# A GRU-like recurrence on one core: TensorE's loop of four steps, x in column tiles, and the z gate of the second half in a group of its own

## The chip, the core and the metric

The program runs on one core of a Trainium2 chip. The metric is the device time of one execution in microseconds. Engines are named as in the profile: PE is TensorE (PEld its weight loads), DVE VectorE, ACT ScalarE, POOL GpSimd, SP the engine that issues the DMAs.

## What is computed

For a batch of 8 sequences of 512 steps with 512 features, all in float32:

```python
def step(h, x_t):
    fused = sigmoid(concatenate([x_t, h], -1) @ w_W + w_b)      # 1024 x 1024
    r, z = split(fused, 2, axis=-1)
    m = x_t @ wx_W + wx_b + r * (h @ wh_W + wh_b)               # 512 x 512 each
    h_new = z * h + (1.0 - z) * tanh(m)
    return (h_new, h_new)
out = x + scan(step, h0, x over time)
```

Each step needs the h of the step before it, so 512 steps follow one another. The products with x do not depend on h.

## The kernel before

The 512 features lie as 128 partitions x 4 chunks (`KC`); the four chunks are two halves (`HALVES`), 0 ("A") and 1 ("B"). A step's products with h are 3 gates (r, m, z) x 512 outputs. h is the stationary operand (128 rows x 8 columns, the batch), the weights `wh` move, and four column tiles of the array (`tile_position=(0, 32*j)`, `TILES` = 4) work at the same time, each on a quarter of the outputs. A matmul of the program on float32 is two matmuls and two weight loads in the trace.

The outputs are cut into groups, each in its own bank of `ps`, (first column, columns, bank): `RM_A` (r and m of half A, 128 columns), `RMZ_B` (r, m and z of half B, 192) and `Z_A` (z of half A, 64). A call `products(group, half, s)` adds the part of one half of h to a group; it is 8 matmuls of the program, 16 in the trace. PE's step is: wait for h of half A, RM_A and RMZ_B with half A of h; wait for half B of h, RM_A with half B (done: `rm_a_done`), Z_A with both halves (`z_a_done`), RMZ_B with half B (`rmz_b_done`). That is 96 matmuls in the trace, on line 192.

After it PE does some of the products with x, for the next block of 16 steps (`STEPS`). Here `wx` is stationary, 128 x 128 over the whole array, and x moves, 128 columns (16 steps x 8). `x_list` holds 48 of these per block, and `X_PLAN` gives 3 or 4 of them to each of the steps 0 to 14 and none to step 15; in the trace they are line 181, x6 or x8 a step. The address of x in `x_sb` depends on the loop's counter. ACT takes the finished units out of PSUM (line 228) and places a step's x part in `add` (line 233).

DVE's step, in order, with the trace's lines: turn (a 32x32 transpose out of PSUM) of r and m of A, line 284; `sum_r` (288); turn of z of A; `sum_z` (292); `mix_m` (298, a scan that gives r*(hW+b)+x); turn of r and m of B; `mix_h` of A (307, a scan that writes h and frees PE by `h_ready[0]`); `sum_r` of B; turn of z of B; `sum_z`, `mix_m`, `mix_h` of B (`h_ready[1]`). ACT answers with sigmoids (237, 241) and the tanh (246) that `mix_h` needs. POOL adds the bias to the m product (362) and makes y = x + h (375). Both `mix_m` wait for POOL and ACT, and both `mix_h` for ACT.

All engines run their own loop of 32 blocks of 16 steps written out. SP loads x for the block after the next and stores y once per block. Every engine executes its instructions in the order written; there is no scheduler.

Of the kernel before, what the change touches and what calls it, by code (L numbers as in the profile page):

```python
# [5 lines left out]
ALU = mybir.AluOpType  # L6
ACT = mybir.ActivationFunctionType

P = 128
# [3 lines left out]
def build(nc, x, h0, w_h, w_x, b_x, b_h, out):  # L13
# [6 lines left out]
    STEPS = 16  # L20
    BLOCKS = T // STEPS
    TOK = STEPS * B
    UNITS = HALVES * GATES * HC
    Y_HALF = STEPS // 2
# [7 lines left out]
    X_FROM = [-(-len(x_list) * s // (STEPS - 1)) for s in range(STEPS)] + [len(x_list)]  # L32
    X_PLAN = [x_list[X_FROM[s]:X_FROM[s + 1]] for s in range(STEPS)]
    X_ENDS = [[u for u, k in plan if k == KC - 1] for plan in X_PLAN]

# [3 lines left out]
    RMZ_B = (P, P + P // 2, 1)  # L39
    Z_A = (2 * P + P // 2, P // 2, 2)  # L40
    GROUP_BANKS = 3
# [12 lines left out]
    with ctx:  # L54
# [9 lines left out]
        x_sb = sb("x_sb", [P, KC, T * B])  # L64
        wx = sb("wx", [P, UNITS, KC, P])
# [5 lines left out]
        h = sb("h", [P, STEPS, HALVES, HALF])  # L71
        y = sb("y", [P, KC, STEPS, B])
# [13 lines left out]
        def h_of(s, k):  # L86
            o, ci = divmod(k, HC)
            at = 1 + TRI * B * ci + 1
            return h[:, s, o, at:at + TRI * (B - 1) + 1:TRI]
# [13 lines left out]
        x_loaded = sem("x_loaded")  # L103
        y_stored = sem("y_stored")
# [7 lines left out]
        rmz_b_done = sem("rmz_b_done")  # L112
# [4 lines left out]
        x_product = sem("x_product")  # L117
        r_summed = halves("r_summed")
# [20 lines left out]
        def _(sp):  # L139
            sp.sem_inc(y_stored, 16)  # L140
            x_flat = x.rearrange("p c t b -> p c (t b)")
            out_flat = out.rearrange("p c t b -> p c (t b)")
            sp.dma_start(x_sb[:, :, 0:TOK], x_flat[:, :, 0:TOK]).then_inc(x0_loaded, 16)  # L143
# [11 lines left out]
            def store(i):  # L155
                sp.wait_ge(y_added, sp.snap(i * STEPS + 2 * STEPS))
                sp.sem_inc(y_taken, 1)
                sp.dma_start(out_flat[:, :, bass.ds(sp.snap(i * TOK), TOK)],
                             y[:, :, :, :].rearrange("p c t b -> p c (t b)")).then_inc(y_stored, 16)

            with sp.Fori(0, BLOCKS - 2) as i:
                sp.wait_ge(x_loaded, sp.snap(i * 16 + 16))
                cols = bass.ds(sp.snap(i * TOK + 2 * TOK), TOK)
                sp.dma_start(x_sb[:, :, cols], x_flat[:, :, cols]).then_inc(x_loaded, 16)
                store(i)
            sp.wait_ge(x_loaded, (BLOCKS - 1) * 16)
            sp.sem_inc(x_loaded, 16)
            with sp.Fori(BLOCKS - 2, BLOCKS) as i:
                store(i)
            sp.wait_ge(y_stored, 16 * (BLOCKS + 1))  # L170

        @block.tensor
        def _(pe):
            def x_products(plan, i_next, unit0):
                for u, k in plan:
                    if k == 0 and not (isinstance(unit0, int) and unit0 + u < 2):
                        pe.wait_ge(xg_ready, unit0 + (u - 1))
                    cols = slice(0, TOK) if isinstance(i_next, int) else bass.ds(i_next * TOK, TOK)
                    if isinstance(i_next, int) and k == 0 and u * WX_PARTS % UNITS == 0:
                        pe.wait_ge(wx_loaded[u * WX_PARTS // UNITS], 16)  # L180
                    mm = pe.matmul(ps[:, X_BANK + u % 2, 0:TOK], wx[:, u, k, :], x_sb[:, k, cols],  # L181
                                   start=(k == 0), stop=(k == KC - 1))
                    if k == KC - 1:
                        mm.then_inc(x_product, 1)
# [256 lines left out]
```

## Time and profile before

| | us |
|---|---|
| median of 3 runs | 1894.34 (1892.4 to 1894.72) |
| the profiled execution, whole | 1895.98 |
| its span, first to last instruction | 1893.4 |
| PE busy (98% of the span) | 1859.9 |
| DVE busy (62%) | 1169.8 |
| ACT busy (43%) | 821.2 |
| POOL busy (20%) | 371.0 |

Of the profiled execution, 2.6 us lie outside the span. The granted TensorE clock has a mean of 0.998 over the span. A busy PE is a PE with a matmul in flight; several overlap, so that the share says little of how full the array is.

### The profile page before, as it was taken

Reading aid. Unit: us, or ns where it says so; the run is one execution under the profiler, and the core shown is the slowest. Engines: PE = TensorE matmul, PEld = TensorE weight load, DVE = VectorE, ACT = ScalarE, POOL = GpSimd, SP = SyncE. Lnnn points to the kernel's source line nnn. Section 1 sums busy time; section 2 is a strip of 40 time slices with the busy share of each in tenths; the row PEclk is TensorE's granted clock in tenths of the full one; section 3 lists DMA queues with packets and bytes.
Section 4 is the critical chain, followed back from the end, with each engine's and each line's share of the span. In section 5 each row is a group of like instructions: output and inputs, shape, how many; then the busy total and the mean of one; then the engine's idle time right before and its main releaser. Section 6 shows DMA issues by size and latency. Waiting matters only on the chain.

```text
span 1893.4 us, 124703 instructions
## 1 busy us (share of the span) xinstructions
PE 1859.9 (98%) x52320; PEld 1465.7 (77%) x52320; DVE 1169.8 (62%) x6153; ACT 821.2 (43%) x3983; POOL 371.0 (20%) x1540
## 2 busy tenths in 40 slices
PE   8999999999999999999999999999999999999998
PEld 6777777777777777777777777777777777777776
DVE  3666666666666666666666666666666666666665
ACT  3444444444444444444444444444444444444444
POOL 0111111111111111111111111111111111111111
PEclk9999999999999999999999999999999999999999
DMA  4000000000000000000000000000000000000000
GB/s 152 15 4 15 15 15 15 9 9 15 15 15 15 4 15 15 15 15 4 15 15 15 15 9 9 15 15 15 15 4 15 15 15 15 4 15 15 9 9 9
DMA packets 36083, 29.94 MB, mean 16 GB/s; under 512 B 1616, under 2 KB 34384, under 8 KB 35664
## 3 DMA queue, kind: packets, MB, share of 16 engines
q1 hardware_dynamic: 35664, 23.10, 3.9%
q8 instruction: 416, 6.82, 1.5%
q14 instruction: 3, 0.02, 0.0%
HBM read 14.70 MB, written 8.39 MB: 12 GB/s over the span
## 4 chain that ended last, share of the span: by engine, by line
PE 96%; DVE 2%; DMA 1%; ACT 1%; SPq 0%; issue 0%; POOL 0%; POOLq 0%
PE ps L192 73%; PE ps L181 23%; DVE turned L284 1%; DMA x_sb<-in_x 1%; DVE h L307 0%; ACT h_by L241 0%; DVE pre_z L292 0%; DVE pre_r L288 0%; ACT h L246 0%; SPq L146 0%; SPq L152 0%; SPq L143 0%; SPq L150 0%; SPq L148 0%; SPq L149 0%
## 5 line engine op out<-in xcount | busy, mean ns | idle before, releaser
L192 PE MATMUL ps<-wh,h 128*8 128x128 f32 (+2 forms) x49152 | 1443.2, 273 | 22.5 <-DVE h L307 19.2
L192 PEld LDWEIGHTS ps<-wh,h 128*8 128x8 f32 x49152 | 1073.4, 90 | 260.1 <-DVE h L307 44.0
L284 DVE STREAM_TRANSPOSE turned<-ps 128x128 f32<-128x128 f32 (+1 forms) x2048 | 575.1, 281 | 510.6 <-PE ps L192 483.6
L237 ACT ACTIVATE m_by<-pre_r 128x16 f32<-128x16 f32 x1024 | 223.4, 218 | 894.5 <-DVE pre_r L288 894.5
L181 PEld LDWEIGHTS ps<-x_sb,wx 128*128 128x128 f32 x3168 | 392.3, 192 | 161.8 <-issue 161.8
L181 PE MATMUL ps<-x_sb,wx 128*128 (+1 forms) x3168 | 483.9, 292 | 5.6 <-DMA wx<-in_w_x 5.6
L362 POOL TENSOR_TENSOR add<-turned,bias_h 128x16 f32<-128x16 f32 x1024 | 237.4, 232 | 881.4 <-DVE turned L284 881.4
L307 DVE TENSOR_TENSOR_SCAN h<-h_by,h 128x48 f32<-128x48 f32 x1024 | 263.5, 257 | 152.9 <-ACT h L246 152.6
L241 ACT ACTIVATE h_by<-pre_z 128x16 f32<-128x16 f32 x1024 | 230.2, 225 | 160.0 <-DVE pre_z L292 131.2
L375 POOL TENSOR_TENSOR y<-x_sb,h 128x32 f32<-128x32 f32 x512 | 133.4, 261 | 637.5 <-DVE h L307 637.5
L246 ACT ACTIVATE h<-m_pre 128x32 f32<-128x32 f32 x1024 | 237.6, 232 | 0.0
L298 DVE TENSOR_TENSOR_SCAN m_pre<-m_by,add 128x32 f32<-128x32 f32 x1024 | 224.7, 219 | 0.0
L292 DVE TENSOR_TENSOR pre_z<-turned,add 128x16 f32<-128x16 f32 x1024 | 179.6, 175 | 35.0
L288 DVE TENSOR_TENSOR pre_r<-turned,add 128x16 f32<-128x16 f32 x1024 | 167.1, 163 | 17.4
L228 ACT ACTIVATE xg<-ps,bias_x 128x128 f32 (+1 forms) x396 | 145.5, 367 | 9.3 <-PE ps L181 9.1
L233 ACT ACTIVATE add<-xg 128x96 f32 (+1 forms) x513 | 145.5, 284 | 0.1
L338 DVE MEMSET ps<- 128x1536 f32 x1 | 1.3, 1338 | 1.2 <-PEq L433 1.2
L350 DVE COPY h<-h 128x8 f32<-128x8 f32 x4 | 0.4, 168 | 2.5 <-DMA h<-in_h 2.5
L267 ACT ACTIVATE warm<-bias_h 128x4 f32<-128x4 f32 x1 | 0.2, 205 | 3.8 <-DMA bias_h<-in_b_h 3.8
L267 ACT ACT_TABLE_LOAD x1 | 1.3, 1283 | 0.7 <-PEq L433 0.7
L341 DVE MEMSET h<- 128x1600 f32 x1 | 1.4, 1392 | 0.3 <-issue 0.3
L433 POOL MEMSET const-float32-0.0<- 128x1 f32 x1 | 0.1, 99 | 0.2 <-issue 0.2
(6 smaller groups left out, 0.6 us busy)
## 6 DMA issues: line engine op xcount, KB each, us to landing
x_sb<-in_x SPq DMA_DIRECT2D x32, 256.0 KB, 4.6
out_h<-y SPq DMA_DIRECT2D x32, 256.0 KB, 2.7
wx<-in_w_x SPq DMA_DIRECT2D x6, 512.0 KB, 5.8
wh<-in_w_h SPq DMA_DIRECT2D x4, 768.0 KB, 11.3
bias_x<-in_b_x SPq DMA_DIRECT2D x1, 6.0 KB, 3.2
bias_h<-in_b_h SPq DMA_DIRECT2D x1, 2.0 KB, 3.1
h<-in_h SPq DMA_DIRECT2D x1, 16.0 KB, 3.6
```

The costliest lines, as they stand in the source:

```text
L181: mm = pe.matmul(ps[:, X_BANK + u % 2, 0:TOK], wx[:, u, k, :], x_sb[:, k, cols], start=(k == 0), stop=(k == KC - 1))
L192: mm = pe.matmul(ps[Q * j:Q * j + B, bank, 0:cols], h_of(s - 1 if s else S, k), wh[:, k, j, at:at + cols], start=(k == 0), stop=(k == KC - 1),
L228: act.activation(dst, ps[:, X_BANK + u % 2, 0:TOK].rearrange("p (t b) -> p t b", b=B), ACT.Identity, bias=bias_x[:, u:u + 1]).then_inc(xg_ ...
L237: act.activation(m_by[:, o, :, 1], pre_r[:, o, :], ACT.Sigmoid).then_inc(r_ready[o], 1)
L241: act.activation(h_by[:, o, :, 2], pre_z[:, o, :], ACT.Sigmoid).then_inc(z_ready[o], 1)
L246: act.activation(n_twice, m_pre[:, o, :, 1].unsqueeze(2).to_broadcast([P, HB, 2]), ACT.Tanh)\
L284: return dve.transpose(turned[:, o, g0:g1].rearrange("p g c q -> p (g c) q"), ps[:, bank, at:at + cols].rearrange("p (c q) -> p c q", q=Q))
L288: dve.tensor_tensor(pre_r[:, o].rearrange("p (c b) -> p c b", b=B), product_of(o, R), x_of(par, o, R), ALU.add).then_inc(r_summed[o], 1)
L292: dve.tensor_tensor(pre_z[:, o].rearrange("p (c b) -> p c b", b=B), product_of(o, Z), x_of(par, o, Z), ALU.add).then_inc(z_summed[o], 1)
L298: dve.tensor_tensor_scan(m_pre[:, o].rearrange("p i w -> p (i w)"), m_by[:, o].rearrange("p i w -> p (i w)"), add[:, par, o, M].rearrange( ...
L307: dve.tensor_tensor_scan(h[:, s, o, 0:REGION], h_by[:, o].rearrange("p i w -> p (i w)"), h[:, s - 1 if s else S, o, 1:1 + REGION], 0.0, AL ...
L362: pool.tensor_tensor(add[:, par, o, M, :, 0].rearrange("p (c b) -> p c b", b=B), product_of(o, M), bias_h[:, HC * o:HC * (o + 1)].unsqueez ...
```

## The change

PE's loop is four steps (`RING` = 4) and runs 128 times, where it was sixteen steps and ran 32 times. All addresses in it are fixed: the x weights of each step come by DMA into one of four places `wx_step` (three 128 x 128 blocks a step, 192 KB), the x of the next block lies four times in `x_next`, and h is a ring of four. SP issues these loads: one `wx_step` each step, and one `x_next` in each of the last four steps of a block. y gets two buffers. Each step has exactly three x products, step 15 too, and each is four matmuls in column tiles of 32 stationary columns, the cut that the products with h have. The x units go round three PSUM banks instead of two.

`RMZ_B` is split into `RM_B` (128 columns) and `Z_B` (64 columns, bank 3). PE computes Z_B last, both halves after RM_B is done. DVE does `sum_r` of B ahead of `mix_h` of A, and turns z of B after it. DVE waits for POOL's y additions every four steps, and for all of them up to the step before; it was every eight, with eight steps of lag. POOL waits for the load of `x_sb` at each block's start, where PE did.

The diff, cut to its core:

```diff
-    X_FROM = [-(-len(x_list) * s // (STEPS - 1)) for s in range(STEPS)] + [len(x_list)]
-    X_PLAN = [x_list[X_FROM[s]:X_FROM[s + 1]] for s in range(STEPS)]
+    X_EACH = len(x_list) // STEPS
+    X_UNITS = RING * X_EACH // KC
...
-    RMZ_B = (P, P + P // 2, 1)
-    Z_A = (2 * P + P // 2, P // 2, 2)
+    RM_B = (P, P, 1)
+    Z_A = (2 * P, P // 2, 2)
+    Z_B = (2 * P + P // 2, P // 2, 3)
...
+            for r in range(RING):
+                load_wx(r)
+                sp.dma_start(x_next[:, r], x_flat[:, :, TOK:2 * TOK]).then_inc(x_next_loaded[r], 16)
             sp.dma_start(x_sb[:, :, TOK:2 * TOK], x_flat[:, :, TOK:2 * TOK]).then_inc(x_loaded, 16)
...
+            def x_product_of(u, k, w, moving):
+                for j in range(TILES):
+                    at = slice(Q * j, Q * (j + 1))
+                    mm = pe.matmul(ps[at, X_BANK + u % X_UNITS, 0:TOK], w[:, at], moving,
+                                   start=(k == 0), stop=(k == KC - 1), tile_position=(0, Q * j))
...
+            def x_products(i, s):
+                pe.wait_ge(wx_step_loaded[s], held(pe, i * 16 + 16))
+                pe.wait_ge(x_next_loaded[s], held(pe, (i // (STEPS // RING)) * 16 + 16))
+                for n in range(X_EACH):
+                    u, k = divmod(s * X_EACH + n, KC)
+                    if k == 0:
+                        pe.wait_ge(xg_ready, held(pe, i * X_UNITS + (UNITS - X_UNITS + u + 1)))
+                    last = x_product_of(u, k, wx_step[:, s, n, :], x_next[:, s, k, :])
...
                 pe.wait_ge(h_ready[0], nxt)
                 products(RM_A, 0, s)
-                pe.wait_ge(z_b_turned, nxt)
-                products(RMZ_B, 0, s)
+                products(RM_B, 0, s)
                 pe.wait_ge(h_ready[1], nxt)
                 products(RM_A, 1, s).then_inc(rm_a_done, 1)
                 products(Z_A, 0, s)
                 products(Z_A, 1, s).then_inc(z_a_done, 1)
-                products(RMZ_B, 1, s).then_inc(rmz_b_done, 1)
+                products(RM_B, 1, s).then_inc(rm_b_done, 1)
+                pe.wait_ge(z_b_turned, nxt)
+                products(Z_B, 0, s)
+                products(Z_B, 1, s).then_inc(z_b_done, 1)
...
-            with nc.Fori(0, BLOCKS, engines=(mybir.EngineType.PE,), hint_back_edge=True) as i:
+            with nc.Fori(0, T // RING, engines=(mybir.EngineType.PE,), hint_back_edge=True) as i:
...
-                if s % Y_HALF == 0:
-                    dve.wait_ge(y_added, held(dve, t0 + (s + Y_HALF)))
+                if s % RING == 0:
+                    dve.wait_ge(y_added, held(dve, t0 + (s + STEPS)))
...
+                pool.wait_ge(x_loaded, pool.snap(i * 16 + 16))
```

PE, one step inside the loop. Before (step 1 of the block; `8x192` is a matmul with 8 stationary and 192 moving columns, in the program's own count, half of the trace's):

```order
L192 MATMUL ps<-wh,h 8x128 [waits h_ready0]
L192 MATMUL ps<-wh,h 8x128 x7
L192 MATMUL ps<-wh,h 8x192 [waits z_b_turned]
L192 MATMUL ps<-wh,h 8x192 x7
L192 MATMUL ps<-wh,h 8x128 [waits h_ready1]
L192 MATMUL ps<-wh,h 8x128 x7
L192 MATMUL ps<-wh,h 8x64 x16
L192 MATMUL ps<-wh,h 8x192 x8
```

After, the last step of the loop's body with the loop's end:

```order
L232 MATMUL ps<-wh,h 8x128 [waits h_ready0]
L232 MATMUL ps<-wh,h 8x128 x15
L232 MATMUL ps<-wh,h 8x128 [waits h_ready1]
L232 MATMUL ps<-wh,h 8x128 x7
L232 MATMUL ps<-wh,h 8x64 x16
L232 MATMUL ps<-wh,h 8x128 x8
L232 MATMUL ps<-wh,h 8x64 [waits z_b_turned]
L232 MATMUL ps<-wh,h 8x64 x15
L200 MATMUL ps<-x_next,wx_step 32x128 [waits x_next_loaded3,wx_step_loaded3]
L200 MATMUL ps<-x_next,wx_step 32x128 x11
L256 REGISTER_ALU
L256 COMPARE_AND_BRANCH
```

The 64 columns of z of B moved from the 192-column matmuls to the end, and the branch now stands behind x products. Before, the branch stood right behind step 15's products with h, and step 0 began with a wait for h:

```order
L192 MATMUL ps<-wh,h 8x64 x16
L192 MATMUL ps<-wh,h 8x192 x8
L213 REGISTER_ALU
L213 COMPARE_AND_BRANCH
L54 UNCONDITIONAL_BRANCH
```

DVE, middle of a step, before:

```order
L298 SCALAR_TENSOR_TENSOR m_pre<-m_by,add 128x32 [waits hm_ready0,r_ready0]
L284 STREAM_TRANSPOSE turned<-ps 128x128 [waits rmz_b_done]
L307 SCALAR_TENSOR_TENSOR h<-h_by,h 128x48 [waits z_ready0,tanh_ready0]
L288 TENSOR_TENSOR pre_r<-turned,add 128x16 [waits rm_b_turned]
L284 STREAM_TRANSPOSE turned<-ps 128x64
```

and after:

```order
L338 SCALAR_TENSOR_TENSOR m_pre<-m_by,add 128x32 [waits hm_ready0,r_ready0]
L324 STREAM_TRANSPOSE turned<-ps 128x128 [waits rm_b_done]
L328 TENSOR_TENSOR pre_r<-turned,add 128x16 [waits rm_b_turned]
L347 SCALAR_TENSOR_TENSOR h<-h_by,h 128x48 [waits z_ready0,tanh_ready0]
L324 STREAM_TRANSPOSE turned<-ps 128x64 [waits z_b_done]
```

`pre_r` of B moved ahead of the h of A, and the last turn waits for a group of its own.

## Rows read from the trace of the kernel before

**Rows 1.** the page: span, first part, and the instruction queue of part 3
```profile
span 1893.4 us, 124703 instructions
...
PE 1859.9 (98%) x52320; PEld 1465.7 (77%) x52320; DVE 1169.8 (62%) x6153; ACT 821.2 (43%) x3983; POOL 371.0 (20%) x1540
...
q8 instruction: 416, 6.82, 1.5%
```

**Rows 2.** the chain of work in time, 901.4 to 920: start us, us, what
```profile
901.51 1.09 PE ps L181 x8
902.60 2.74 PE ps L192 x96
905.34 0.86 PE ps L181 x6
```

**Rows 3.** waits, whole run: engine line, waited for, us in total, times, longest us
```profile
PEld ps L181 <- issue: 161.8, 481, 5.6
```

**Rows 4.** timeline of a covered step: start us, us, what [idle before]
```profile
905.27 0.74 PEld L181 LDWEIGHTS ps<-x_sb,wx 128*128 128x128 f32 x6 [0.33 <-issue]
...
906.13 2.81 PE L192 MATMUL ps<-wh,h 128*8 128x128 f32 x96
...
907.91 0.32 DVE L284 STREAM_TRANSPOSE turned<-ps 128x128 f32<-128x128 f32 x1 [0.88 <-PE ps L192]
...
908.88 0.94 PE L181 MATMUL ps<-x_sb,wx 128*128 x6
```

**Rows 5.** timeline of the uncovered step, 897 to 900.5, same columns
```profile
897.01 0.32 DVE L284 STREAM_TRANSPOSE turned<-ps 128x128 f32<-128x128 f32 x1 [0.88 <-PE ps L192]
897.36 0.18 DVE L288 TENSOR_TENSOR pre_r<-turned,add 128x16 f32<-128x16 f32 x1
...
897.46 0.25 DVE L284 STREAM_TRANSPOSE turned<-ps 128x64 f32<-128x64 f32 x1
...
897.83 0.22 DVE L298 TENSOR_TENSOR_SCAN m_pre<-m_by,add 128x32 f32<-128x32 f32 x1
...
898.08 0.23 ACT L246 ACTIVATE h<-m_pre 128x32 f32<-128x32 f32 x1
898.11 0.32 DVE L284 STREAM_TRANSPOSE turned<-ps 128x128 f32<-128x128 f32 x1
898.35 0.26 DVE L307 TENSOR_TENSOR_SCAN h<-h_by,h 128x48 f32<-128x48 f32 x1
...
898.52 0.15 DVE L288 TENSOR_TENSOR pre_r<-turned,add 128x16 f32<-128x16 f32 x1
898.59 0.24 DVE L284 STREAM_TRANSPOSE turned<-ps 128x64 f32<-128x64 f32 x1
...
898.66 2.85 PE L192 MATMUL ps<-wh,h 128*8 128x128 f32 x96 [0.62 <-DVE h L307]
...
899.47 0.26 DVE L307 TENSOR_TENSOR_SCAN h<-h_by,h 128x48 f32<-128x48 f32 x1 [0.30 <-ACT h L246]
899.78 1.33 PEld L192 LDWEIGHTS ps<-wh,h 128*8 128x8 f32 x64 [0.24 <-DVE h L307]
899.97 0.27 POOL L375 TENSOR_TENSOR y<-x_sb,h 128x32 f32<-128x32 f32 x1 [1.22 <-DVE h L307]
...
900.48 0.32 DVE L284 STREAM_TRANSPOSE turned<-ps 128x128 f32<-128x128 f32 x1 [0.75 <-PE ps L192]
```

**Rows 6.** back edge, by line: durations min/median/max ns, first and last start
```profile
L213 PEldq ALU_OP  x1: 32/32/32, 897.2 to 897.2; - x1
L213 PEldq COMPARE_BRANCH  x1: 375/375/375, 897.3 to 897.3; - x1
...
L199 PEldq ALU_OP  x1: 36/36/36, 897.9 to 897.9; - x1
...
L353 DVEq COMPARE_BRANCH  x1: 61/61/61, 899.6 to 899.6; - x1
```

**Rows 7.** timeline: the second half's h of the first and the last step
```profile
28.92 0.26 DVE L307 TENSOR_TENSOR_SCAN h<-h_by,h 128x48 f32<-128x48 f32 x1 [0.30 <-ACT h L246]
...
1889.44 0.26 DVE L307 TENSOR_TENSOR_SCAN h<-h_by,h 128x48 f32<-128x48 f32 x1 [0.30 <-ACT h L246]
```

**Rows 8.** the page, part 6: KB each, median us from issue to landing
```profile
wx<-in_w_x SPq DMA_DIRECT2D x6, 512.0 KB, 5.8
```

More of the change, by code:

```diff
@@ L20, in build @@
     STEPS = 16
+    RING = 4
     BLOCKS = T // STEPS
@@ L103, in build @@
         x_loaded = sem("x_loaded")
+        x_next_loaded = [sem(f"x_next_loaded{r}") for r in range(RING)]
+        wx_step_loaded = [sem(f"wx_step_loaded{r}") for r in range(RING)]
         y_stored = sem("y_stored")
@@ L117, in build @@
         x_product = sem("x_product")
+        x_used = [sem(f"x_used{r}") for r in range(RING - 1)]
         r_summed = halves("r_summed")
@@ L167, in _ @@
[L167 to L170, printed above, removed]
+                             y[:, bass.ds(sp.snap(i % 2), 1)].rearrange("p a c t b -> p (a c) (t b)"))\
+                    .then_inc(y_stored, 16)
+            sp.wait_ge(x_loaded, (BLOCKS + 1) * 16)
+            for r in range(RING):
+                sp.wait_ge(wx_step_loaded[r], (T // RING + 1) * 16)
+                sp.wait_ge(x_next_loaded[r], (BLOCKS + 1) * 16)
@@ L172, in _ @@
+            sp.wait_ge(y_stored, 16 * (BLOCKS + 2))
         @block.tensor
         def _(pe):
[L174 to L179, printed above, removed]
-                        pe.wait_ge(wx_loaded[u * WX_PARTS // UNITS], 16)
[L181 to L184, printed above, removed]
+            def x_product_of(u, k, w, moving):
[3 more added lines that the diff above has]
+                                   start=(k == 0), stop=(k == KC - 1), tile_position=(0, Q * j))
+                if k == KC - 1:
+                    mm.then_inc(x_product, 1)
+                return mm
@@ new lines, in first_x_products @@
+            def first_x_products():
+                for u, k in x_list:
+                    if k == 0 and u >= X_UNITS:
+                        pe.wait_ge(xg_ready, u - X_UNITS + 1)
+                    if k == 0 and u * WX_PARTS % UNITS == 0:
+                        pe.wait_ge(wx_loaded[u * WX_PARTS // UNITS], 16)
+                    x_product_of(u, k, wx[:, u, k, :], x_sb[:, k, 0:TOK])
+            def x_products(i, s):
[6 more added lines that the diff above has]
+                    last = x_product_of(u, k, wx_step[:, s, n, :], x_next[:, s, k, :])
+                if s < RING - 1:
+                    last.then_inc(x_used[s], 1)
@@ L364, in hidden, with add_x @@
                     .then_inc(hm_ready[o], 1)
-            def add_x(s, t0, nxt, after):
+            def add_x(s, t0, which, after):
                 if s == 0:
@@ L382, in step @@
                     hidden(o, s % 2, nxt)
-                add_x(s, t0, nxt, held(pool, t0 + (s + 2)))
+                add_x(s, t0, which, held(pool, t0 + (s + 2)))
             pool.sem_inc(y_added, STEPS)
```

97 lines of the change are left out of this document (54 added, 43 removed).

## The prediction, made before the changed kernel ran

> **What bounds the kernel now.** I read the page first: PE has a matmul in flight for 98% of the span, the other engines are far below [rows 1]. Then the chain of waits in order of time: it runs through PE for step after step, 2.74 us of products with h and 0.86 us of products with x, 3.60 us a step, or 0.86 + 0.23 where eight x matmuls stand instead of six [rows 2]. So PE sets the pace of 15 of 16 steps. The span holds 511 steps between the end of the first h of half B (28.92 + 0.26 = 29.18) and of the last (1889.70) [rows 7]: 1860.5 / 511 = 3.641 us a step. Around them lie 29.2 us at the start, 1893.4 - 1889.7 = 3.7 at the end and 1895.98 - 1893.4 = 2.6 outside the span.
>
> The row that matters most is the one step that PE does not bound. Step 15 has no x products, so PE stands idle 0.62 us for the h of half A [rows 5]. From one turn of r and m of A to the next it takes 900.48 - 897.01 = 3.47 us. That is the length of the recurrence itself: turn, sum, sigmoid, scan, tanh, scan, for A and then B, and PE's products back to the turn. Whatever PE gains, the step does not get under this loop unless the loop changes too. The slack is 3.641 - 3.47 = 0.17 us a step, 87 us in all.
>
> **PE's own time.** x in column tiles. Before each x phase the weight loader stands idle 0.33 us [rows 4], 481 times and 161.8 us in total [rows 3], for no semaphore: with the array full of column tiles the first full-width load waits. In the chain [rows 2], eight x matmuls take 1.09 us and six 0.86, so one costs (1.09 - 0.86) / 2 = 0.115 us, six cost 0.69, and 0.17 of the 0.86 is the switch; some 0.12 more hides in the end of the 2.74, as drain. With x in the cut of the h products both go. The six become 24 of 32 columns, in sets of four that stream the same 128 columns: 0.69 us, if four loads of 32 columns cost together what one of 128 does. The h products keep their 384 columns per part of h; 32 more matmuls in the trace cost a few ns each. PE alone: 2.74 + 0.69 = 3.43 at most, 3.31 if the drain of 0.12 is gone. I take 3.31. Step 15 now has its x products too, and the eights become sixes. So PE falls below the recurrence of 3.47, and the recurrence becomes the bound.
>
> The Trainium skill has a sentence on this, in "TensorEngine Tiling (Array Packing)", section "Key Properties": changing the tiling mode, not only the tile, drains the engine. The trace has the 0.33 us in front of every change to full width, and nothing of the kind between h groups.
>
> **The recurrence after the change.** I write T for the start of the turn of r and m of A and walk along DVE's order with the intervals of [rows 5]. Before: `sum_r` at 0.35, turn of z at 0.45, `mix_m` at 0.82, turn of B at 1.10, h of A at 1.34 (the tanh ends at 1.30), `sum_r` of B 1.51, turn of z of B 1.58, h of B 2.46, its end 2.72, next turn 3.47, which is 0.75 us after the end of h.
> After, up to `mix_m` nothing changes: RM_A and Z_A are done at the same distance. The turn of B comes earlier. It stood at 1.10 since the 192-column products of `RMZ_B` ended then; with 128 columns they end 0.2 us earlier (a third of 16 matmuls at 2.74 / 12288 us per column: 1024 columns, 0.23). Then the scan `mix_m` is the bound: DVE starts an instruction about 0.08 before the end of the one ahead if it waits for nothing (898.59 against 898.52 + 0.15), so 0.82 + 0.22 - 0.08 = 0.96. `sum_r` of B waits for all of that turn: 0.96 + 0.35 = 1.31. Now h of A stands behind it: 1.31 + 0.10 = 1.41, not 1.34, a loss of 0.07. The turn of z of B follows 0.17 behind h of A (898.52 - 898.35), at 1.58; before, `sum_r` stood between and it was 1.58 too. Gain and loss cancel, and from there nothing changes: h of B ends at 2.72, the next turn is at 3.47. If the turn of B stays at 1.10, as an upper bound, everything after it shifts by 0.14 and the step is 3.61, a gain of almost nothing.
>
> Z_B stands last on PE and is no wait: before, 5120 columns stood behind RM_A and x began 908.88 - 907.91 = 0.97 after T, the drain in it [rows 4]. Now it is 6144 columns: 1024 more are 0.22, and the drain of 0.12 goes or stays, so x begins at T + 1.07 to 1.19, and z of B is turned at 1.58. x ends at 1.76 to 1.88. RM_A and RM_B with half A of h are a third of the h products, 0.87 to 0.91, and end at 2.63 to 2.79; h of B is there at 2.72 and its first load starts 0.05 later (899.78). The two meet almost at one time. PE then waits 0 to 0.14 us a step, and the steps have little cover left for anything late on PE.
>
> **The back edge.** The loop turns 128 times instead of 32. PE's sequencer takes from 897.2 to 897.9 + 0.04 for it, 375 ns of that in the branch, where DVE's takes 61 [rows 6]. Before, this lay under the wait for h. It was begun when the matmuls of the last group, 16, were still ahead of the array. With the same lead, it begins now 16 matmuls of x (0.44 to 0.46 us) before the end of x, at about T + 1.31; 0.77 us later PE can take the first matmul, at 2.1 to 2.15 with its start, and with 0.88 for RM_A and RM_B it is ready for h of B at 3.02 instead of 2.79: 0.23 us an edge, 127 edges, 29 us. The lower bound: the instruction queue moved 6.82 MB, which is 65 bytes for each of the 104,640 matmuls and loads that PE executed and only 55 for each of all 124,703 instructions [rows 1]. I read that as PE's loop fetched anew each time round, and the other engines' smaller loops kept. If PE's short loop is kept too and the branch costs what DVE's does, the edge takes 0.3 less and costs 0 to 0.05 us: 0 to 6 us. Nothing in the trace shows which, so I take the middle, 0.14 us, 18 us in all. The Trainium skill ("Runtime: NRT & Kernel Launch", section "Instruction fetch mechanics") gives PE room for 2048 instructions; by that the new loop of some 1,250 would fit and the old one of some 3,300 would not, if what was fetched is kept at all, and the sum would be 1809 to 1815. The same section calls that memory a FIFO without a cache's reuse, by which the edge would cost as before or more.
>
> **The rest.** DVE waits every four steps for the y addition of the step before. POOL starts it 899.97 - (899.47 + 0.26) = 0.24 after h of B and takes 0.27; it is done 0.51 after h, the turn is at 0.75. Cover 0.24, cost 0; it would take a POOL half as slow again to show. SP issues one load a step more, three of them ahead, so that each has some 10 us, where 512 KB land in 5.8 [rows 8]: 0. At the start `x_sb` of block 1 is queued behind 1.8 MB more and POOL waits for it, but PE no longer does; I set 0, with 0 to 5 us for the range. At the end, the last loads stand before the store: 0 to 1 us.
>
> **Sum.** 29.2 + 511 x 3.47 + 18 + 3.7 + 2.6 = 29.2 + 1773.2 + 24.3 = 1826.7 us, against 1895.98 of the profiled execution, which lies 1.6 above the median. Rounded with that: 1826.
>
> **Rivals.**
> *The turn of B doesn't come early enough*: it stays between 0.96 and 1.10, since the order on DVE or the end of RM_B holds it. The steps take 3.54 to 3.61 and PE has slack that hides the back edge: 29.2 + 511 x 3.61 + 6.3 = 1880, or 1850 in the middle. For it: DVE now stands idle nowhere between `mix_m` and h of A. Against: RM_B's end is reckoned at 0.9. Chance 0.18.
> *PE still bounds and the recurrence gets shorter*, by something that I put down as fixed: 29.2 + 511 x 3.31 + 6.3 = 1727, plus edges. Against it speaks that every interval in the loop was seen at 3.47 with no PE in the way. 0.05.
> *Slower by the loads of column tiles.* If a load of 32 columns isn't hidden behind its own tile's matmuls, a set of four takes 0.11 + 0.11 us, the x phase 1.3 instead of 0.69 and PE 3.93: 29.2 + 511 x 3.93 + 6.3 = 2044. It decides from 0.17 us a set on, where PE reaches 3.64. Against: the narrow loads of 8 columns are hidden even behind 64-column matmuls. 0.08.
> *Slower by the fetch at the back edge.* The instruction queue was busy 1.5% of 16 engines' span for 416 packets, 1.1 us each [rows 1]. If every edge stalls for one such packet beyond the 0.77 us seen, it costs 0.23 + 1.1 = 1.33 us, 169 in all: 1809 + 169 = 1978. It decides from 0.68 us an edge on, where 127 edges eat the 87 us. Against: the branch of before went as far back and took 375 ns. 0.06. The same section of the Trainium skill has the rule: a taken branch to a place outside the window that is held forces a fetch before the engine goes on.
> That the change doesn't do what it says (the loads of `wx_step` late, PE waiting for them) I give 0.01; it would be seen as waits for DMA.
>
> **How the numbers follow.** The forecast (recurrence 3.47, edge 0 to 0.23, some us at the start) holds 0.62 and gives 1808 to 1845. The first rival takes it on to 1880. Together 0.80, so the range is 1806 to 1882. What it leaves out is 0.15 above and 0.05 below. A measurement can tell about 0.2% from no change, 3.8 us. Faster: 0.62 + 0.18 + 0.05, less 0.01 for a first rival that eats the whole gain: 0.84. Slower: 0.08 + 0.06 + 0.01 = 0.15. Same: 0.01; I give it 0.02 and faster 0.83.
>
> **What the new profile would show.** The 0.33 us of idle weight loader before x gone, and no idle time above 0.1 there. PE's waits for the h of half B in nearly each step, up to 0.14 us, and DVE and ACT in the chain of every step. Turn to turn 3.47 in three steps of four and 3.5 to 3.7 in the one with the branch. The turn of B 0.96 after the turn of A, h of A at 1.41. The instruction queue tells which edge it is: some tens of packets (kept) or some 600. Wrong would be: PE with no waits (a set of four above 0.15 us, or something on PE that I don't see), turn B at 1.1, or DVE waiting for POOL's y.

## The result, and the profile after

| | before | after |
|---|---|---|
| median | 1893.87 us (4 runs) | 1808.78 us (4 runs, 1807.97 to 1809.14) |
| ratio | | 0.9551 (0.9534 to 0.9567) |
| span of the profiled run | 1893.4 | 1806.1 |
| matmuls in the trace | 52,320 | 78,208 |
| mean step, from the end of the first h of B to the end of the last | 3.641 | 3.464 |

The kernel is 4.5% faster, 85 us. The prediction was 1826 with a range of 1806 to 1882, and its sum without the price for the back edge was 1809; 1808.78 lies 3 us inside the lower end of that range. The page, for [rows 1]:

```profile
span 1806.1 us, 178513 instructions
...
PE 1787.5 (99%) x78208; PEld 1629.9 (90%) x78208; DVE 1160.5 (64%) x6153; ACT 824.9 (46%) x3983; POOL 357.1 (20%) x1540
...
q8 instruction: 7, 0.11, 0.0%
...
PE 98%; SPq 1%; DMA 0%; issue 0%; DVE 0%; ACT 0%; POOL 0%; POOLq 0%; DVEq 0%
```

PE has half as many matmuls again and is as busy by this count as before. The instruction queue moved 7 packets where it had moved 416. The chain is PE's at 98%, and that is misleading: it follows PE back at nearly every joint, since PE and the h of B arrive nearly together there. The prediction had expected DVE and ACT in the chain of every step, and that sign did not come. What sets the pace is seen in the timeline of one step, DVE and PE (start us, us, what [idle before]), the counterpart of [rows 5]:

```profile
902.87 0.32 DVE L324 STREAM_TRANSPOSE turned<-ps 128x128 f32<-128x128 f32 x1 [0.82 <-PE ps L232]
903.22 0.17 DVE L328 TENSOR_TENSOR pre_r<-turned,add 128x16 f32<-128x16 f32 x1
...
903.31 0.24 DVE L324 STREAM_TRANSPOSE turned<-ps 128x64 f32<-128x64 f32 x1
...
903.68 0.22 DVE L338 TENSOR_TENSOR_SCAN m_pre<-m_by,add 128x32 f32<-128x32 f32 x1
...
903.82 0.29 DVE L324 STREAM_TRANSPOSE turned<-ps 128x128 f32<-128x128 f32 x1
...
903.99 0.60 PEld L200 LDWEIGHTS ps<-x_next,wx_step 128*32 128x32 f32 x24
...
904.15 0.18 DVE L328 TENSOR_TENSOR pre_r<-turned,add 128x16 f32<-128x16 f32 x1
...
904.24 0.28 DVE L347 TENSOR_TENSOR_SCAN h<-h_by,h 128x48 f32<-128x48 f32 x1
...
904.44 0.22 DVE L324 STREAM_TRANSPOSE turned<-ps 128x64 f32<-128x64 f32 x1
...
904.67 2.90 PE L232 MATMUL ps<-wh,h 128*8 128x128 f32 x128
...
905.30 0.26 DVE L347 TENSOR_TENSOR_SCAN h<-h_by,h 128x48 f32<-128x48 f32 x1 [0.29 <-ACT h L286]
...
905.61 1.78 PEld L232 LDWEIGHTS ps<-wh,h 128*8 128x8 f32 x96 [0.17 <-DVE h L347]
...
906.31 0.32 DVE L324 STREAM_TRANSPOSE turned<-ps 128x128 f32<-128x128 f32 x1 [0.75 <-PE ps L232]
```

From T = 902.87: turn of B at 0.95, `sum_r` of B at 1.28, h of A at 1.37, turn of z of B at 1.57, h of B at 2.43, the next turn at 3.44. The weight loader waits 0.17 us for the h of B (905.61) after RM_A and RM_B with half A; there is no idle time in front of the x products any more, where it was 0.33 [rows 4]. Between 100 and 1700 us, some 460 steps, the waits are (engine, for whom, us in total, times, longest):

```profile
PEld ps L232 <- DVE h L347: 102.2, 492, 0.3
PEld ps L200 <- issue: 3.3, 22, 0.2
```

The first row is the new wait, 492 waits of 0.21 us, 0.22 us a step, where the prediction had at most 0.14. The second stands for the 161.8 us of [rows 3], and is down to 3.3.

The back edge, for [rows 6] (duration in ns min/median/max, first and last start):

```profile
L256 PEldq COMPARE_BRANCH  x115: 216/216/216, 112.1 to 1689.2; - x115
```

The branch takes 216 ns where it took 375.

### The profile page after: what moved, and what is told of

Read it like the earlier page. It is cut to its first block, busy times and chain, and to the rows that moved or that the text cites. A ratio compares the mean times of both kernels' runs of the same rounds, so it can differ in the third digit from the quotient of the medians.

```text
span 1806.1 us, 178513 instructions
## 1 busy us (share of the span) xinstructions
PE 1787.5 (99%) x78208; PEld 1629.9 (90%) x78208; DVE 1160.5 (64%) x6153; ACT 824.9 (46%) x3983; POOL 357.1 (20%) x1540
## 4 chain that ended last, share of the span: by engine, by line
PE 98%; SPq 1%; DMA 0%; issue 0%; DVE 0%; ACT 0%; POOL 0%; POOLq 0%; DVEq 0%
PE ps L232 78%; PE ps L200 20%; SPq L167 0%; SPq L162 0%; DMA x_sb<-in_x 0%; SPq L153 0%; SPq L159 0%; DVE turned L324 0%; SPq L150 0%; DVE h L347 0%; DVE m_pre L338 0%; SPq L157 0%; SPq L156 0%; SPq L155 0%; DVE pre_r L328 0%
## 5 line engine op out<-in xcount | busy, mean ns | idle before, releaser
L232 PE MATMUL ps<-wh,h 128*8 128x128 f32 (+1 forms) x65536 | 1504.7, 246 | 2.6 <-issue 2.2
L232 PEld LDWEIGHTS ps<-wh,h 128*8 128x8 f32 x65536 | 1324.7, 90 | 143.1 <-DVE h L347 113.5
L324 DVE STREAM_TRANSPOSE turned<-ps 128x128 f32<-128x128 f32 (+1 forms) x2048 | 550.4, 269 | 412.4 <-PE ps L232 412.4
L200 PE MATMUL ps<-x_next,wx_step 128*32 128x128 f32 x12288 | 433.0, 274 | 0.6 <-issue 0.6
L403 POOL TENSOR_TENSOR add<-turned,bias_h 128x16 f32<-128x16 f32 x1024 | 222.8, 218 | 709.9 <-DVE turned L324 681.5
L200 PEld LDWEIGHTS ps<-x_next,wx_step 128*32 128x32 f32 x12288 | 316.1, 110 | 16.2 <-issue 4.3
L416 POOL TENSOR_TENSOR y<-x_sb,h 128x32 f32 x512 | 134.0, 262 | 734.5 <-DVE h L347 734.5
L328 DVE TENSOR_TENSOR pre_r<-turned,add 128x16 f32<-128x16 f32 x1024 | 179.8, 176 | 34.9
L200 PE MATMUL ps<-x_sb,wx 128*32 128x128 f32 x384 | 15.1, 323 | 9.8 <-DMA wx<-in_w_x 6.1
L200 PEld LDWEIGHTS ps<-x_sb,wx 128*32 128x32 f32 x384 | 13.3, 131 | 11.0 <-issue 10.3
```

What stands on the lines that cost most here:

```text
L200: mm = pe.matmul(ps[at, X_BANK + u % X_UNITS, 0:TOK], w[:, at], moving, start=(k == 0), stop=(k == KC - 1), tile_position=(0, Q * j))
L232: mm = pe.matmul(ps[Q * j:Q * j + B, bank, 0:cols], h_of(s - 1, k), wh[:, k, j, at:at + cols], start=(k == 0), stop=(k == KC - 1), tile_po ...
L324: return dve.transpose(turned[:, o, g0:g1].rearrange("p g c q -> p (g c) q"), ps[:, bank, 0:cols].rearrange("p (c q) -> p c q", q=Q))
L328: dve.tensor_tensor(pre_r[:, o].rearrange("p (c b) -> p c b", b=B), product_of(o, R), x_of(par, o, R), ALU.add).then_inc(r_summed[o], 1)
L403: pool.tensor_tensor(add[:, par, o, M, :, 0].rearrange("p (c b) -> p c b", b=B), product_of(o, M), bias_h[:, HC * o:HC * (o + 1)].unsqueez ...
```

## The experiments

All times stand against the kernel before, which ran beside each of them: 1893 to 1895 us. The first variant reads the x of block 0 in every block, so that the x part of its result is that of block 0 from the second block on; PE's number of products is the same. All others compute the whole result.

### The parts one at a time

**Column tiles alone**, on the kernel before:

```diff
-                    mm = pe.matmul(ps[:, X_BANK + u % 2, 0:TOK], wx[:, u, k, :], x_sb[:, k, cols],
-                                   start=(k == 0), stop=(k == KC - 1))
+                    for j in range(TILES):
+                        at = slice(Q * j, Q * (j + 1))
+                        mm = pe.matmul(ps[at, X_BANK + u % 2, 0:TOK], wx[:, u, k, at], x_sb[:, k, 0:TOK],
+                                       start=(k == 0), stop=(k == KC - 1), tile_position=(0, Q * j))
```

> The kernel before, with one edit: the x products go in four column tiles of 32. [...] No split of z of B, no short loop, no new loads. Theory (the full-width x cost PE the switch, and with it gone the recurrence bounds): steps with three x products 3.47 us, the three of 16 with four 3.54, mean 3.49, so 29.2 + 511 x 3.49 + 6.3 = 1819 us (1810 to 1828), the 0.33 us of idle weight loader before x gone. Rival (the gain of the change comes from the split of z and DVE's order, or from the short loop): 1880 to 1894. Rival (narrow loads aren't hidden): over 1900.

Measured: 1953.06 us, ratio 1.0285 (1.025 to 1.0319). Slower. A rival had "over 1900", but for loads that aren't hidden; the trace shows another reason. The page (span, instruction queue), PE's timeline where its loop turns, and the branch (ns):

```profile
span 1953.4 us, 143583 instructions
...
q8 instruction: 514, 8.42, 1.7%
```

```profile
928.80 3.05 PE L194 MATMUL ps<-wh,h 128*8 128x128 f32 x93 [2.40 <-issue]
```

```profile
L215 PEldq COMPARE_BRANCH  x2: 2392/2584/2777, 925.7 to 984.2; - x2
```

PE stands 2.4 us with no semaphore to wait for, and its branch takes 2.6 us instead of 0.375. From one end of h of B to the next, most steps of a block took 3.48 to 3.65 us, as the theory wanted, so the loads of the column tiles are hidden. But the first step of a block, behind the branch, took 5.2 to 7.3 (median 6.35), and some others up to 4.2: mean 3.755. The queue moved 514 packets in 1953.4 us, one in 3.80. My reading was that PE waits for its own instructions. The next run changes nothing but the length of the loop's body.

**The changed kernel with PE's body written out for 16 steps:**

```diff
-            with nc.Fori(0, T // RING, engines=(mybir.EngineType.PE,), hint_back_edge=True) as i:
-                t0 = pe.snap(i * RING)
-                for s in range(RING):
-                    step(t0, s)
-                    x_products(i, s)
+            with nc.Fori(0, BLOCKS, engines=(mybir.EngineType.PE,), hint_back_edge=True) as b:
+                for turn in range(STEPS // RING):
+                    t0 = pe.snap(b * STEPS + turn * RING)
+                    for s in range(RING):
+                        step(t0, s)
+                        x_products(b, turn, s)
```

> The changed kernel with PE's loop body written out for 16 steps instead of four, 32 turns instead of 128; every matmul, wait and place is the same. The instruction queue should go from 7 packets to about 610 (10 MB). Theory (the fetch and the edge lie under other work): 1803 to 1813 us, no change. Rival (the short loop is part of the gain: PE waits for its instructions, or an edge that has to be fetched again costs the 0.23 us that I feared): 1815 us for 31 edges of 0.23 us, more if the fetch between them stalls, since 304 instructions a step are half as many again as before.

Measured: 2506.95 us (2478.94 to 2521.22 in four runs), ratio 1.3254 (1.3192 to 1.3315). The same matmuls, waits and loads cost 700 us more. The page, and PE's waits between 100 and 1700 us:

```profile
span 2477.1 us, 178193 instructions
...
q8 instruction: 642, 10.52, 1.7%
```

```profile
PEld ps L232 <- issue: 367.2, 347, 3.5
```

The loop turns only 21 times in that window, so nearly all of the 347 waits lie inside the body and not at the branch: it is the stream of instructions that is late. 642 packets in 2477.1 us are one in 3.86, with the other loads beside them nearly the same as without (3.80 in the run before). PE executes 156,416 matmuls and loads from 642 packets, 244 from each. At the 3.80 us of the run before, a step of 304 needs 304 / 244 x 3.80 = 4.73 us, and the mean step was 4.78. The kernel before needed a packet in 1893.4 / 416 = 4.55 us and lived 16% under that limit. Column tiles for x alone need 514 packets for 512 steps; at 3.6 us a step that would be one in 3.6, and they are over it.

**The short loop alone**: four steps in PE's body with fixed places and the loads, x in full width, z of B not split and DVE in its old order. Against the changed kernel, cut:

```diff
-                for j in range(TILES):
-                    at = slice(Q * j, Q * (j + 1))
-                    mm = pe.matmul(ps[at, X_BANK + u % X_UNITS, 0:TOK], w[:, at], moving,
-                                   start=(k == 0), stop=(k == KC - 1), tile_position=(0, Q * j))
+                mm = pe.matmul(ps[:, X_BANK + u % X_UNITS, 0:TOK], w, moving,
+                               start=(k == 0), stop=(k == KC - 1))
...
-    RM_B = (P, P, 1)
-    Z_A = (2 * P, P // 2, 2)
-    Z_B = (2 * P + P // 2, P // 2, 3)
+    RMZ_B = (P, P + P // 2, 1)
+    Z_A = (2 * P + P // 2, P // 2, 2)
```

> The kernel before with only the short loop: PE's body has four steps with fixed places and the loads that this needs, x in full width, no split of z of B, DVE's old order. Theory (the short loop gives no time itself, it only makes room for more instructions): PE bounds at 2.74 + 0.86 = 3.60 us or a little more, 1878 to 1892 us, as the kernel with the split but full-width x. Rival (the fetch cost the kernel before something too): below 1870.

Measured: 1881.89 us, ratio 0.994 (0.9925 to 0.9955). A small gain, but its interval leaves out 1. The chain of waits in time shows the pair of before [rows 2], unchanged:

```profile
903.22 0.86 PE ps L196 x6
904.09 2.74 PE ps L228 x96
```

So the short loop itself gives 12 us. The steps say from what: before, three of 16 took 3.83 us (four x products) and one 3.47 (none), and the mean was 3.64; now every step has three, and the mean is 3.61. Above all it is what lets PE have more instructions. With the split but x still in full width (the first piece of that diff alone):

> The changed kernel with x in full width again, 128 stationary columns at a time from the same fixed places; the rest (short loop, ring, split of z of B, loads) stays. Theory: PE needs 2.74 + 0.86 = 3.60 us a step and bounds again, PE idle before x 0.33 us, time 31 + 511 x 3.60 + 7.5 = 1878 us (1865 to 1890). Rival (the split or the short loop made the gain): 1809 to 1830.

Measured: 1892.41 us, ratio 0.9989 (0.9979 to 0.9999); the steps took 3.63 us. PE bounds, as expected, but the time lies outside the expected 1865 to 1890: where PE bounds, the split costs 0.02 us a step, 10.5 us in all against the run above. Without the column tiles the short loop's 12 us and this loss leave almost nothing. Then without the split, with column tiles, the short loop and DVE's old order (cut):

```diff
-                products(RM_B, 1, s).then_inc(rm_b_done, 1)
-                pe.wait_ge(z_b_turned, nxt)
-                products(Z_B, 0, s)
-                products(Z_B, 1, s).then_inc(z_b_done, 1)
+                products(RMZ_B, 1, s).then_inc(rm_b_done, 1)
```

> The changed kernel without the split: r, m and z of B in one group of 192 columns, DVE with h of A ahead of sum_r of B, as before; x in column tiles and the short loop stay. Theory: the recurrence has its old length of 3.475 us where the changed kernel's has 3.444, turn of B at 1.10 instead of 0.96 after the turn of A: 1809 + 511 x 0.03 = 1824 us (1818 to 1832). Rival (the split is worth nothing, PE or another bound holds the 3.44): 1809. Rival (the split is worth much, since PE without it is late for h of B): over 1840.

Measured: 1823.76 us, ratio 0.9622 (0.9606 to 0.9638). 3.475 us in most steps, the length of the uncovered step of before. The parts, added in this order, make up the 85 us: the short loop 12 (1893.87 to 1881.89), the column tiles on it 58 (to 1823.76), the split with its order on DVE 15 (to 1808.78). The column tiles are most of the gain, and without the short loop they are a loss of 58.

And the split with DVE's old order, h of A ahead of `sum_r` of B:

```diff
+                mix_h(0, s, nxt)
                 dve.wait_ge(rm_b_turned, nxt)
                 sum_r(1, par, nxt)
-                mix_h(0, s, nxt)
```

> The changed kernel with h of A ahead of sum_r of B on DVE, as before; the groups of 128 and 64 columns stay. Theory (what the split gives is the earlier turn of B, and the new order of the two is worth nothing): turn of B at 0.96, h of A at 1.34, sum_r of B at 1.51, turn of z of B at 1.58 after the turn of A, as in the changed kernel: 1809 us within 4. Rival (the order is what counts): 1815 to 1825, as without the split.

Measured: 1853.29 us, ratio 0.9785 (0.977 to 0.98). My theory fell, and so did the rival's number: it is 44 us worse than the changed kernel and 30 worse than no split. The timeline:

```profile
901.27 0.32 DVE L324 STREAM_TRANSPOSE turned<-ps 128x128 f32<-128x128 f32 x1 [0.75 <-PE ps L232]
...
902.23 0.29 DVE L324 STREAM_TRANSPOSE turned<-ps 128x128 f32<-128x128 f32 x1
...
902.60 0.22 POOL L403 TENSOR_TENSOR add<-turned,bias_h 128x16 f32<-128x16 f32 x1 [0.71 <-DVE turned L324]
902.62 0.32 DVE L347 TENSOR_TENSOR_SCAN h<-h_by,h 128x48 f32<-128x48 f32 x1
902.85 0.14 DVE L328 TENSOR_TENSOR pre_r<-turned,add 128x16 f32<-128x16 f32 x1
902.92 0.24 DVE L324 STREAM_TRANSPOSE turned<-ps 128x64 f32<-128x64 f32 x1
...
904.81 0.32 DVE L324 STREAM_TRANSPOSE turned<-ps 128x128 f32<-128x128 f32 x1 [0.75 <-PE ps L232]
```

The turn of B is early, at 0.96, and h of A starts at 1.35, but that scan takes 0.32 us where it took 0.26 in [rows 5], and `sum_r` starts 0.23 behind it instead of 0.17. The turn of z of B comes at 1.65, and the step is 3.54.

What makes the scan longer stands on POOL. Since the turn of B is earlier now, POOL's bias addition for B falls on h of A: it starts 0.02 us ahead of the scan. In step 9 of each block the two start almost together, the scan first:

```profile
916.84 0.26 DVE L347 TENSOR_TENSOR_SCAN h<-h_by,h 128x48 f32<-128x48 f32 x1
916.84 0.28 POOL L403 TENSOR_TENSOR add<-turned,bias_h 128x16 f32<-128x16 f32 x1 [0.73 <-DVE turned L324]
917.02 0.15 DVE L328 TENSOR_TENSOR pre_r<-turned,add 128x16 f32<-128x16 f32 x1
```

There the scan takes 0.26 us and the addition 0.28 instead of 0.22, `sum_r` follows in 0.18, and the step is 3.483 instead of 3.54. It is so in 31 steps. In 448 the addition starts just ahead and the scan takes 0.31; in 31 more it starts earlier, and the scan begins 0.05 later and takes 0.26. Whichever of the two comes second ends about 0.06 late. In the changed kernel the addition starts about 0.05 ahead of the scan, which then takes 0.28. So 0.06 of the 0.10 that a step loses is this meeting of two engines. No run moved POOL's addition alone, and what the two share inside the chip is not shown.

### How large a loop may be

Two bodies written out for eight steps: that of the short loop alone (204 matmuls and loads a step), and that of the changed kernel (304). Both have this edit:

```diff
-            with nc.Fori(0, T // RING, engines=(mybir.EngineType.PE,), hint_back_edge=True) as i:
+            with nc.Fori(0, T // RING // 2, engines=(mybir.EngineType.PE,), hint_back_edge=True) as b:
+                for turn in range(2):
```

> The kernel with the short loop alone (x in full width, no split), with PE's body written out for eight steps: about 204 matmuls and loads a step, some 1,650 instructions in the body. It asks how large a body is kept. Theory (a room of 2048 instructions, as the Trainium skill has it for PE, is a cache here): the instruction queue moves 3 to 10 packets and the time stays at 1882 us. Rival (what is kept is less, somewhere above the 1,250 of the changed kernel): over 400 packets, and 1882 to 1900 us, since the kernel before lived with that rate.

Measured: 1883.44 us (one run), with 6 packets:

```profile
q8 instruction: 6, 0.10, 0.0%
```

> The changed kernel with PE's body written out for eight steps: 304 matmuls and loads a step, some 2,450 instructions. Theory (the body is over 2048 and the fetch rate of one packet of 256 instructions in 3.7 to 3.8 us bounds): about 610 packets, 304 / 67 = 4.5 us a step at least, 2300 to 2520 us like the body of 16. Rival (bodies of this size are still kept): under 10 packets and 1809 us.

Measured: 2526.16 us (one run, span 2523.7), with 642:

```profile
q8 instruction: 642, 10.52, 1.9%
```

A body of 204 x 8 = 1,632 matmuls and loads stays, one of 304 x 8 = 2,432 is fetched each time round. The 2048 instructions that the Trainium skill gives for PE ("Runtime: NRT & Kernel Launch", section "Instruction fetch mechanics") lie between the two. The same section calls that memory a FIFO, without a cache's gain from code that lies close together, and says that the pace at which the engine's instructions are issued hides the fetch. Here a body of 1,632 was not fetched again (6 packets in the whole run), and with one of 2,432 PE stood waiting for its instructions.

### How much room PE has

More x products in each step, into a bank that nothing reads, ahead of the second x product of each step (EXTRA is 2):

```diff
+                    for j in range(EXTRA * TILES if n == 1 else 0):
+                        at = slice(Q * (j % TILES), Q * (j % TILES + 1))
+                        pe.matmul(ps[at, 7, 0:TOK], wx_step[:, s, n, at], x_next[:, s, k, :],
+                                  start=True, stop=True, tile_position=(0, Q * (j % TILES)))
```

> The changed kernel with eight more column-tiled matmuls (two sets of four, 0.11 us each) in every x phase, into a bank that nobody reads; it measures how much PE has left under the recurrence. Theory (PE alone takes 3.31 us, the recurrence 3.444): the step becomes 3.31 + 0.22 = 3.53, 1809 + 511 x 0.07 = 1845 us. Rival (PE and the recurrence are in series, no slack): 1809 + 511 x 0.22 = 1921. Rival (PE has more slack than I think): 1809 to 1820.

Measured: 1964.61 us (one run). The edit put in twice what the expectation counted: eight float32 matmuls of the program are sixteen in the trace, four sets of 0.109 us. PE's timeline, with its products with h (L237) and the first of those with x (L201):

```profile
902.77 2.83 PE L237 MATMUL ps<-wh,h 128*8 128x128 f32 x128
905.53 0.43 PE L201 MATMUL ps<-x_next,wx_step 128*32 128x128 f32 x8
...
906.64 2.83 PE L237 MATMUL ps<-wh,h 128*8 128x128 f32 x128
909.28 0.41 PE L201 MATMUL ps<-x_next,wx_step 128*32 128x128 f32 x8
...
910.37 2.83 PE L237 MATMUL ps<-wh,h 128*8 128x128 f32 x128
...
914.10 2.83 PE L237 MATMUL ps<-wh,h 128*8 128x128 f32 x128
...
917.83 2.83 PE L237 MATMUL ps<-wh,h 128*8 128x128 f32 x128
```

The profile lists no wait of PE or its loader between 100 and 1700 us here, so PE alone sets the step. It is 3.73 us in three steps of four (910.37 - 906.64). 3.73 - 4 x 0.109 = 3.29: that is PE alone, where the prediction had 3.31. The changed kernel's step of 3.444 leaves it 0.15. The last step of the loop's body holds the branch, and it too takes 3.73 (917.83 - 914.10): the back edge costs nothing even where PE bounds. The long step is the first of the body, 3.87 (906.64 - 902.77): its x products begin 2.76 us after the products with h, in the others 2.64. In the changed kernel it is the same, 1.20 after the turn of A against 1.08. There PE's sequencer has register instructions for the values of three waits (lines 215, 216 and 220) ahead of the x products, in the other steps a single wait. That these cause the delay was not tried alone.

### The waits for y

Three steps of each block (4, 8 and 12) take 3.508 us where the others take 3.444. End of h of B to the next turn, first such a step, then the first step of a block:

```profile
929.41 0.26 DVE L347 TENSOR_TENSOR_SCAN h<-h_by,h 128x48 f32<-128x48 f32 x1 [0.30 <-ACT h L286]
930.49 0.32 DVE L324 STREAM_TRANSPOSE turned<-ps 128x128 f32<-128x128 f32 x1 [0.82 <-PE ps L232]
```

```profile
915.63 0.26 DVE L347 TENSOR_TENSOR_SCAN h<-h_by,h 128x48 f32<-128x48 f32 x1 [0.30 <-ACT h L286]
916.64 0.32 DVE L324 STREAM_TRANSPOSE turned<-ps 128x128 f32<-128x128 f32 x1 [0.75 <-PE ps L232]
```

929.67 to 930.49 is 0.82 us, 915.89 to 916.64 is 0.75. The second has the back edge of PE and the wait for y as well, so neither explains the difference. In the trace DVE's sequencer first passes the wait for `rm_a_done` as an instruction of its own and the turn carries the wait for y; in the first step of a block it is the other way round, since there the y wait rides on a register instruction. The semaphore that comes last costs 0.07 us more if it stands ahead of the turn and not on it.

```diff
-                if s % RING == 0:
-                    dve.wait_ge(y_added, held(dve, t0 + (s + STEPS)))
                 dve.wait_ge(rm_a_done, nxt)
...
+                if s % RING == 0:
+                    dve.wait_ge(y_added, held(dve, t0 + (s + STEPS)))
                 dve.wait_ge(rm_b_done, nxt)
```

> The changed kernel with DVE's wait for POOL's y additions moved from the start of every fourth step to the turn of r and m of B in the same step, where the ring place it guards is still untouched. In the changed kernel the steps 4, 8 and 12 of a block are 0.065 us longer than their neighbours (3.508 against 3.444), since the turn starts 0.82 us after h of B and not 0.75; in steps 0 it is 0.75. Theory (two waits on one instruction, the later one in front of it): the 96 long steps go to 3.444, 96 x 0.065 = 6 us, 1802.5 us. Rival (POOL's addition itself, or PE's back edge, makes these steps long): no change, 1809, or the delay shows at the turn of B.

Measured: 1812.85 us, ratio 0.957 (0.9557 to 0.9583). The expected 6 us did not come; it is 4 us worse than the changed kernel. The turn of A came 0.75 behind h in all steps, as the theory has it. But in four steps of each block the turn of B now started 0.03 late and took 0.02 more, though both its semaphores had long been set, so that `sum_r` of B was 0.05 late. The second wait costs DVE 0.05 us even where nothing is waited for, if DVE has no gap there. Four steps of 0.05 cancel three of 0.065. The other loss is in step 9 of each block: it takes 3.54 us instead of 3.46, with `mix_m` of A 0.09 late, 32 x 0.08 = 2.6 us. Why is open.

### A kernel that beats both

On DVE, the turn of z of B ahead of h of A:

```diff
-                mix_h(0, s, nxt)
                 dve.wait_ge(z_b_done, nxt)
                 turn(3, 1, Z, GATES).then_inc(z_b_turned, 1)
+                mix_h(0, s, nxt)
```

> The kernel with the y wait moved, and DVE's turn of z of B ahead of h of A: turn of B, sum_r of B, turn of z of B, h of A. Theory (DVE's order sets the recurrence): turn of z of B at 1.38 after the turn of A instead of 1.58, h of A at 1.51 instead of 1.38, sum_z of B at 1.68 instead of 1.83, m of B at 1.77 (its sigmoid is ready at 1.75), h of B ends at 2.55 instead of 2.69. Then h of A, ending at 1.79, and PE bound: 1.84 + 1.56 = 3.40 us a step, 1802.5 - 511 x 0.045 = 1780 us (1765 to 1795). Rival (h of A later makes PE later by as much as B gains): 1800 or above.

Measured: 1780.31 us, ratio 0.9401 (0.9389 to 0.9414), expected 1780. That the number fits so well is luck in part: the expectation started from 1802.5, but the kernel that it builds on took 1812.85, so the gain is 32.5 us where 22.5 was expected. Most steps take 3.38 us, not 3.40; the four with the y wait take 3.44.

```profile
899.88 0.32 DVE L324 STREAM_TRANSPOSE turned<-ps 128x128 f32<-128x128 f32 x1 [0.86 <-PE ps L232]
...
900.84 0.29 DVE L324 STREAM_TRANSPOSE turned<-ps 128x128 f32<-128x128 f32 x1
...
901.26 0.24 DVE L324 STREAM_TRANSPOSE turned<-ps 128x64 f32<-128x64 f32 x1
901.43 0.22 DVE L347 TENSOR_TENSOR_SCAN h<-h_by,h 128x48 f32<-128x48 f32 x1
...
902.15 0.26 DVE L347 TENSOR_TENSOR_SCAN h<-h_by,h 128x48 f32<-128x48 f32 x1 [0.30 <-ACT h L286]
903.27 0.32 DVE L324 STREAM_TRANSPOSE turned<-ps 128x128 f32<-128x128 f32 x1 [0.86 <-PE ps L232]
```

Turn of B at 0.96, turn of z 1.38, h of A 1.55, end of h of B 2.53 after T = 899.88. The next turn comes 0.86 behind h of B, not 0.75: the loop now runs over h of A, which ends at 1.77, and PE's 1.57 us from there to the turn. Then the y wait where DVE has 0.1 us to spare, off the turn of B, behind h of A and every third step:

```diff
                 mix_h(0, s, nxt)
+                if s % 3 == 0:
+                    dve.wait_ge(y_added, held(dve, t0 + (s + STEPS)))
                 dve.wait_ge(z_b_turned, held(dve, t0 + (s + 2)))
```

> The kernel that turns z of B ahead of h of A (1780 us), with the wait for POOL's y taken off the turns: it stands after h of A, ahead of sum_z of B, every third step, where h of B has 0.1 us to spare. Theory (a second wait costs DVE 0.05 to 0.07 us where it stands, whether it waits or not, and nothing where DVE has slack): the four long steps of each block go from 3.44 to 3.38, 128 x 0.06 = 7.5 us, 1773 us. Rival (the slack is not there): 1780 or more.

Measured: 1775.39 us, ratio 0.9374 (0.9362 to 0.9387). The steps are at 3.38 now, but for the first of every four, from its turn of A to the next, at 3.427. It is not the back edge, which lies in the step before and costs nothing: in the first step of PE's body the x products begin 1.19 us after the turn of A and not 1.08, as in the run with more matmuls, and now 0.05 of that reaches the h products of the next step.

## Why the prediction was right, point by point

**The bound moves from PE to the recurrence: right.** The length of the loop was read in one step of the kernel before, 3.47 us, and the new kernel has 3.444 in nearly all steps without a y wait. The walk along DVE came out within 0.04 us: turn of B 0.95 (0.96), `sum_r` 1.28 (1.31), h of A 1.37 (1.41), turn of z 1.57 (1.58). The 0.03 is the turn of 128 columns: behind another instruction it takes 0.29 us, not 0.32, and I took the interval from one that had stood idle. That is 511 x 0.026 = 13 us by which the forecast was too high.

**PE alone 3.31: right**, 3.29 by the run with more matmuls, 3.43 in the first step of the loop's body, which the prediction did not see. The narrow loads are hidden: the x phase runs with no idle loader.

**The back edge, 18 us in the sum: the mis-sized term.** It costs nothing: the first step of a block has the edge and takes 3.445, like its neighbours, and with PE as the bound the step that holds the branch takes 3.73, again like its neighbours. The lower bound was the case. The loop is kept, 7 packets, and the branch takes 216 ns. The prediction looked for 3.5 to 3.7 us in the step with the branch; three of four such steps do take 3.508, but by the y wait, so that sign fitted by chance.

**The y wait, 0 us: wrong.** POOL was in time, as reckoned, but I did not count that two waits at one instruction cost time by themselves. 96 x 0.065 = 6 us.

**Start and end, 0 us: somewhat wrong.** The first h of B ended at 31.0 us instead of 29.2, since POOL waited for the x behind the new loads, as the prediction named it:

```profile
POOL add L403 <- DMA x_sb<-in_x: 28.4, 1, 28.4
...
DVE m_pre L338 <- POOL add L403: 1.8, 1, 1.8
```

28.4 us of waiting, until after the first turn, and 1.8 us that `mix_m` then waited for POOL. The four steps after it, in which PE ran through its loop's body for the first time, took 3.9 to 4.4 us: 16.67 - 4 x 3.444 = 2.9 us more. The end took 4.9 us instead of 3.7.

The sum with the measured terms: 1826.7 - 13 - 18 + 6 + 1.8 + 2.9 + 1.2 = 1807.6, against 1807.97 of the profiled run. So the forecast was 31 us too high in two terms and 12 too low in four, and part of its nearness is that these cancel.

**The reason that was missed.** The prediction priced the fetch of instructions at the back edge alone, and weighed whether it costs 0 to 29 us, or 169 as a rival. What the short loop saves is not the edge. It is the stream: with a body that has to be fetched, 304 matmuls and loads a step take 4.8 us, whatever the edge costs. The rows for it were there, 416 packets in 1893.4 us, but with no sign how near that was to the limit; only the runs showed 3.8 us a packet. Both bounds on the edge assumed a stream that keeps up. That the prediction was right on the time rests on the change having the short loop already, and on PE keeping it; the prediction left open whether it does.

**The split.** The expected gain and loss on DVE did cancel to within 0.03 us, but those 0.03 are the 15 us that the split is worth, which the sum had at nothing. It pays only with `sum_r` first; with h of A first it costs 30.

## What to carry to other kernels

Find the length of the recurrence in a step in which the busiest engine has nothing else to do; that number, not the busy share, says what relief on that engine can bring. Before adding instructions to PE's loop, count them: a body of some 1,600 matmuls and loads was kept here, one of 2,400 was fetched each turn, and then a packet of about 244 instructions takes 3.8 us and that is the bound. On an in-order engine without gaps, a second semaphore wait is an instruction of 0.05 to 0.07 us even where nothing is waited for, so it belongs where the engine has slack. When an instruction of one engine moves, look for what it now meets on another: the steps of one trace that differ in this alone can tell the price.

## What the runs showed of the hardware that I had not expected

- The instruction fetch of PE has a rate: 3.80, 3.86 and 3.93 us a packet in the three runs that were bound by it, though a packet itself takes 1.0 to 1.2 us on its queue (medians); 4.55 in the kernel before, which did not need more. A PE that is short of instructions shows idle time put down to "issue", and a branch of 2.6 us (median of two, in the run with column tiles alone).
- The branch of a kept body takes 216 ns in the changed kernel and 221 in the short loop alone, that of a fetched one 375 in the kernel before, where the stream keeps up. The edge of the kept body added nothing to a step even with PE as the bound.
- The turn of 128 columns out of PSUM takes 0.32 us after idle time and 0.29 directly behind another instruction. The h scan takes 0.26 us with POOL idle, 0.31 where POOL's addition starts just ahead of it, and then the addition its usual 0.22; where the scan starts first it takes 0.26 and the addition 0.28. In the two kernels that turn z of B first, where POOL's addition is over by then, it takes 0.22.
